# Weight loads that wait for gathered rows, and row numbers copied during a landing wait

## The reference

```
x = x + x-by-feature times w0[cond[b]]             # 64 x 64 matrix chosen per sequence
x = x + attention(x, paged keys and values)         # window of 256, 8 heads, 4 kv heads of 64
x = x + x @ W[id[b]] + b[id[b]]                     # one of 16 experts, 512 x 512 floats each
x = x + x @ W3.T + low-rank term of adapter[b]      # rank 16, one of 8
```

## Time and profile before

| | us |
|---|---|
| median of three timed runs | 1178.34 |
| lowest and highest | 1176.82, 1183.21 |
| profiled execution | 1169.61 |
| its span, first to last instruction | 1167.8 |
| first block | about 0 to 305 |
| second block | about 309 to 1167 |
| TensorE busy | 1050.6 |
| mean granted TensorE clock | 0.950 |

### The profile page before, as it was taken

One profiled execution on the slowest core, in us unless ns is written; L12 is line 12 of the kernel. 1 busy time (PEld: TensorE's weight loads), 2 busy tenths in 40 slices (PEclk: granted clock), 3 DMA queues, 4 the chain that ended last, 5 costly groups with the idle time before them and its releaser, 6 DMA issues. The chain is left out here.

```text
span 1167.8 us, 23800 instructions
## 1 busy us (share of the span) xinstructions
PE 1050.6 (90%) x6440; PEld 713.3 (61%) x6440; DVE 654.7 (56%) x1888; ACT 535.0 (46%) x1336; POOL 535.5 (46%) x597
## 2 busy tenths in 40 slices
PE   4999999999247979999999979999999999999997
PEld 2767677877124655666656646666666666666655
DVE  5889795377333535555555534555555555555552
ACT  3457765475133424544444433444444444444440
POOL 1545444245545454554454445454455554555400
PEclk9999998899666979999999989999999999999998
DMA  3343443353263646665566655656666566665640
GB/s 125 116 137 134 141 147 112 110 167 138 84 198 89 186 149 204 212 214 187 176 205 210 207 168 168 187 182 196 201 227 196 179 201 203 222 195 179 204 145 19
DMA packets 95336, 196.15 MB, mean 168 GB/s; under 512 B 31346, under 2 KB 40114, under 8 KB 87110
## 3 DMA queue, kind: packets, MB, share of 16 engines
q1 hardware_dynamic: 63942, 149.49, 37.9%
q0 software_dynamic: 30784, 44.16, 14.2%
q10 hardware_dynamic: 576, 2.10, 0.5%
HBM read 195.08 MB, written 33.56 MB: 196 GB/s over the span
## 5 line engine op out<-in xcount | busy, mean ns | idle before, releaser
L981 POOL DMA_INDIRECT KV<-kv_scratch,idxs x192 | 190.6, 993 | 290.4 <-DMA KV<-in_pool,idxs 251.4
L971 POOL DMA_INDIRECT KV<-in_pool,idxs x192 | 193.7, 1009 | 107.4 <-issue 81.8
L1130 DVE CUSTOM_DVE_ANT_0 SM<-bank,FM 128x336 f32<-128x336 f32 x256 | 129.8, 507 | 192.8 <-PE bank L1246 171.8
L1052 ACT ACTIVATE PT<-bank 112x384 f32<-112x384 f32 x256 | 111.9, 489 | 264.8 <-PE bank L1254 264.3
L1061 ACT ACTIVATE PR<-SM,nb 128x336 f32<-128x336 f32 x256 | 145.8, 577 | 0.8 <-DVE nb L1134 0.6
L1267 PE MATMUL bank<-PT,KV 112*64 112x128 f32 x1536 | 113.3, 283 | 17.3 <-ACT PT L1052 17.3
L1052 ACT ACTIVATE KT<-bank 128x336 f32<-128x336 f32 x128 | 57.6, 450 | 154.5 <-PE bank L1233 154.5
L1267 PEld LDWEIGHTS bank<-PT,KV 112*64 112x64 f32 x1536 | 86.1, 139 | 65.3 <-issue 40.5
L1292 PE MATMUL bank<-W,XT 128*64 128x512 f32 x512 | 123.7, 604 | 0.7 <-ACT XT L1052 0.7
L90 PE MATMUL bank<-wqh,XTH 128*128 128x512 f32 x256 | 108.0, 422 | 9.2 <-DVE XTL L480 8.5
L1246 PE MATMUL bank<-KT,QB 64*128 64x336 f32 x512 | 111.1, 512 | 5.6 <-ACT KT L1052 5.1
(11 more groups left out here) (157 smaller groups left out, 1934.6 us busy)
## 6 DMA issues: line engine op xcount, KB each, us to landing
W<-in_w SPq DMA_DIRECT2D x64, 1024.0 KB, 8.4
FM<-mask SPq DMA_DIRECT2D x64, 168.0 KB, 4.0
X<-in_x SPq DMA_DIRECT2D x32, 256.0 KB, 2.8
x_scratch<-X SPq DMA_DIRECT2D x32, 256.0 KB, 2.1
kv_scratch<-KVR SPq DMA_DIRECT2D x32, 256.0 KB, 2.5
qt_scratch<-QT SPq DMA_DIRECT2D x32, 256.0 KB, 2.8
QB<-qt_scratch SPq DMA_DIRECT2D x32, 256.0 KB
XB<-x_scratch SPq DMA_DIRECT2D x32, 256.0 KB
```

Of the source, the lines that this page charges most:

```text
L971: pool.indirect_dma_start(out=KV[k][:, c, :], out_offset=None, in_=t["pool"], in_offset=bass.IndirectOffsetOnAxis(ap=idxs[k][:, c:c + 1], ...
L981: pool.indirect_dma_start(out=KV[k][:, c, :], out_offset=None, in_=kv_d, in_offset=bass.IndirectOffsetOnAxis(ap=idxs[k][:, NCH + c:NCH + c ...
L1052: return nc.scalar.activation(dst, src, ACT.Copy)
L1130: v.tensor_tensor_reduce(out=SM[u % 2][:, :], in0=bank[u % 2][:, 0:SPAN], in1=FM[k][:, :], scale=1.0, scalar=-3e38, op0=ALU.add, op1=ALU.m ...
```

## The change

```diff
@@ -950,6 +950,13 @@
 
             @block.gpsimd
             def _(pool):
+                def places(pr, b):
+                    k, n = 2 * pr.par + b, pr.n * 2 + b
+
+                    wait_all(pool, s_pass_pool, (s_new[k], 16 * NCH * pr.i))
+                    nc.gpsimd.tensor_copy(idxs[k][:, :], idxT[:, :, bass.ds(n, 1)].rearrange("p a o -> p (a o)")
+                                          ).then_inc(s_reg[k], 1)
+
                 def body(pr, attention, dense, adapted):
                     if not attention:
                         return
@@ -960,11 +967,7 @@
                         return 8 * (p - 2) + 4 * (b + 1)
 
                     def held(b):
-                        k, n = 2 * pr.par + b, p * 2 + b
-
-                        wait_all(pool, s_pass_pool, (s_new[k], 16 * NCH * pr.i))
-                        nc.gpsimd.tensor_copy(idxs[k][:, :], idxT[:, :, bass.ds(n, 1)].rearrange("p a o -> p (a o)")
-                                              ).then_inc(s_reg[k], 1)
+                        k = 2 * pr.par + b
 
                         wait_all(pool, s_pass_pool, (s_pv, used(b)), (s_reg[k], at(pr.i, 1, 0)))
                         for c in range(NCH):
@@ -983,10 +986,15 @@
                                 in_offset=bass.IndirectOffsetOnAxis(ap=idxs[k][:, NCH + c:NCH + c + 1], axis=0),
                                 bounds_check=NB * T - 1, oob_is_err=False).then_inc(s_new[k], 16)
 
-                    for b in range(2):
-                        held(b)
-                        fresh(b)
-
+                    held(0)
+                    places(pr, 1)
+                    fresh(0)
+                    held(1)
+                    if not last_pair(pr):
+                        places(pr.move(1), 0)
+                    fresh(1)
+
+                places(Pair(0, 0), 0)
                 bodies(pool, body)
 
             @block.sync
@@ -1014,9 +1022,15 @@
                 def body(pr, attention, dense, adapted):
                     p = pr.n
 
+                    def landed(b):
+                        ahead = pr.move(1 + b)
+                        if not (isinstance(p, int) and ahead.n >= PAIRS):
+                            wait(sp, s_old[2 * ahead.par + 1 - b], at(ahead.i, 16 * NCH, 16 * NCH - 1))
+
                     def weights(b):
                         e = sp.value_load(eid[0:1, bass.ds(p * 2 + b, 1)], min_val=0, max_val=E - 1)
                         wait(sp, s_l2, p - 1)
+                        landed(b)
                         sp.dma_start(W2[pr.par][b][:, :], w2_v[bass.ds(e, 1)]).then_inc(s_w2in[pr.par][b], 16)
```

## The result

The changed kernel took 1173.07 us (median of 20 runs, 1164.41 to 1186.32), and the kernel before, run beside it on the same chip, 1184.38 (median of 20, 1176.82 to 1204.67). The ratio is 0.9927, with a 95% interval of 0.9904 to 0.9949: faster by 11 us, where the forecast took off 26.5. The profiled execution took 1164.41 us, 5.2 less than that of before (1169.61); its span is 1162.6.

A forecast was written before the change was run, and what follows sets the result against it. TensorE was taken to be held up by late gathered rows, GpSimd's chain having no slack. Two lone waits and the start, 11.5 + 12.0 + 3 = 26.5 us, off 1178.3 gave 1152, range 1141 to 1174.

The forecast's parts named there:

- What bounds the kernel, and the price of a lone wait: Second block: TensorE waits for late gathered rows; the two lone waits cost 11.5 and 12.0 us, low clock included.
- The copy and the weights' wait: GpSimd's chain and SyncE's weights: 0.8 us saved per half pair, landings 3.3 and 4.0, both lone waits gone, -23.5 us.
- What queues behind that wait: SyncE's queue behind the waiting weights: nothing moves in a steady body; masks land 3.7 to 6.6 us after issue.
- The start: Second block's start: pair 1's rows come earlier, its `scores` at 354 to 357; gains 1 to 4 us, taken as 3.
- The sum: Whole kernel: 11.5 + 12.0 + 3 = 26.5 us off the profiled execution and off the timed median.
- What is late next is TensorE's own work, so undisturbed bodies stay at 24.3 us: Second block's steady stream: with the lone waits gone, TensorE's own work sets each body, 24.3 us.
- Taking the same off gives 1152: Timed median: the 26.5 us taken off 1178.3 leave 1152; forecast chance 0.62.
- the timed runs held more stalls than the profile: Rival, timed runs: the 8.7 us above the profile are nearly one more stall, also removed, giving 1143; chance 0.10.
- The slower case, every gather in a weight's tail: Rival, second block: every gather meets a weight's tail, landings 5.7 us each, bodies 26.4, giving 1211; chance 0.11.

The follow-up runs named there:

- e1: The changed kernel with only the row-number copies moved, the weights not waiting for landings; 1151.18 us, ratio 0.9813 to the kernel before.
- e4: The changed kernel again, unedited, on the first chip; 1142.33 us, ratio 0.9745 to the kernel before.
- e12: The changed kernel with only the row-number copies moved, no weights' wait, on the third chip; 1180.41 us, ratio 0.9992 to the kernel before.
- e2: The changed kernel with only the weights' wait, the row-number copy put back ahead of the old rows; 1175.86 us, ratio 1.0024 to the kernel before.
- e11: The changed kernel a fourth time, unedited, on the third chip; 1173.4 us, ratio 0.9909 to the kernel before.
- e7: The changed kernel a third time, unedited, on the second chip; 1171.88 us, ratio 0.9836 to the kernel before.
- e8: The kernel before, unedited, traced on the second chip; 1185.07 us, ratio 1.0014.
- e9: The changed kernel with weight loads from pair 2 on cut to 256 of 2048 columns; 1176.61 us, ratio 0.9897 to the kernel before.

## Why the prediction was right in its mechanism and wrong in its size

**What bounds the kernel, and the price of a lone wait: right.** The two stalls went; they had cost 35.79 - 24.29 = 11.5 and 36.28 - 24.36 = 11.9 us, and e1 showed a third one of the same price, 11.8.

**The copy and the weights' wait: right as a pair.** GpSimd catches up (18 waits for `values` in e4 against 10 in the earlier trace rows; the 43 of after count longer bodies too), and in e4 the weights stand alone, half a body apart, at 360.89 and 371.56 for the first such pair. The landings of e4 were 3.7 us on average, with 6.3 the longest, where I took 3.3 and 4.0. On the first chip each part alone did less: 26 us off for the copy, none for the wait, 35 for both. On the third the copy alone did nothing (e12).

**What queues behind that wait: right only with the moved copy.** I had found that "in a steady body nothing behind it moves". That held in e4. In e2, with an unmoved copy, queries and masks were issued when they were before, within half a microsecond, but landed late behind a weight that had started 2 us ahead of them, in steady bodies, and the whole gain of the wait was lost.

**The start: wrong, 3 us forecast, none seen.** The first three bodies took 82.56 us in e4 and 82.6 before (324.73 to 407.33). The rows came earlier as worked out, and pair 1's `scores`, forecast for 354 to 357, began at 355.40. What was left out is the body after. The first three bodies of before, then the first and the third of e4:

```profile
324.73:407.33 82.60, 60.93 (x378) 37.56 (x378) 33.84 (x124) 33.14 (x91) 38.23 (x44) 0.78 0.52 160
```

```profile
324.00:355.40 31.40, 17.95 (x84) 10.68 (x83) 9.45 (x37) 11.42 (x29) 18.58 (x21) 0.50 0.41 120
...
380.97:406.56 25.59, 25.20 (x163) 16.51 (x164) 13.17 (x46) 10.97 (x31) 12.56 (x14) 0.94 0.67 191
```

The first body is 1.4 us longer than before (the queries, issued at 347.89), the second 2.8 shorter although it ends in a second wait for queries of 2.41 us, and the third 1.3 longer. That third body has almost no idle time: it runs at a mean granted clock of 0.94 where before had 1.00, right after that second wait. So TensorE stood idle 4.4 us less over the three bodies than before, and was busy 4.3 us longer with the same 378 matmuls at a lower mean clock. I had priced the queue behind the held weight for one body and not for the second, and had put no term for the clock there.

**The sum: 26.5 forecast, 27.0 measured from profile to profile, partly by luck.** e4 against before: the first `scores` 0.7 us earlier, the first four bodies 11.5 less, the next 27 another 11.5, and the end, from the last `scores` on, 3.2. That last term was in no forecast. It is clock alone, the same 270 matmuls at a mean granted clock of 0.93 and of 1.00. Before, then e4:

```profile
1112.68:1167.80 55.12, 45.92 (x270) 31.44 (x269) 20.72 (x61) 13.79 (x37) 0.00 (x0) 0.93 0.23 81
```

```profile
1088.88:1140.80 51.92, 42.73 (x270) 28.86 (x269) 20.73 (x61) 13.79 (x37) 0.00 (x0) 1.00 0.25 87
```

**The step that failed** is "What is late next is TensorE's own work, so undisturbed bodies stay at 24.3 us", together with "Taking the same off gives 1152". On the first chip the first is true, 24.37 us a body, and the median came out even lower than the second says, at 1142.33. In the runs after the prediction, and on two other chips, what was late next was the hand-over from TensorE to ScalarE, VectorE and GpSimd. It made the bodies 25.06 us in after (25.5 in e11: 687.7 us for 27), which is 19 us over 27 bodies more than the 24.36 of the trace that the forecast was made from. Late hand-overs put time into the bodies of either kernel: 27 bodies took 676.7 us in after, 687.7 in e11, 699.9 in e7 (whose profiled execution was its longest), and 688.1 in the kernel before (e8). That alone would leave the difference between the two kernels as it was. What shrinks it is that the longer bodies rescue the chain of before by themselves. In e8 there is one lone stall in place of two, and the copy alone gives a ratio of 0.9992 and not 0.9813. That longer bodies are what takes the stalls away rests on one profile of the kernel before there (e8) and on e12; I haven't lengthened a body on purpose on the first chip to show it.

**The rivals.** That the timed runs held more stalls than the profile (1143) gives the median of the first chip, 1142.33, and there the kernel before is spread from 1164.98 to 1199.57 us and the changed one within 2.3. No trace of a run of before with more stalls was taken on that chip, so its mechanism is not shown. No lone wait for fresh rows was found in the changed kernel's steady stream. The slower case, every gather in a weight's tail, did not come: 64 landing waits took 213.9 us in after, 3.3 each (with the copy's 0.2 us now ahead of the wait), against 251.4 and 3.9 before, and it would have needed 5.7.

## What to carry to other kernels

When a queue is made to wait for a landing, list what stands behind the waiting instruction and move what is needed soonest ahead of it; the version with early queries had the lower median both times that it ran beside the changed kernel (1163.5 against 1171.9 us, 1167.0 against 1173.4), though the intervals overlap. What is issued right behind a large load on the same queue can be late even if it is issued on time (e2). A stall that comes from a chain with no slack seems to be worth its price only where the rest of the kernel is as short as in the profile: where bodies ran 1 us longer, the chain caught up without the change in the one profile of it (e8). So read a second profile of the kernel before, from another chip, before adding up such stalls.

## What the runs showed of the hardware

One program took 1142.33 us on one chip (1141.53 to 1143.82) and 1171.88 and 1173.4 on two others; each chip was seen in one batch only, so chip and hour can't be told apart. In the traces of the two others, and in after, waits behind TensorE end later after the recorded end of the matmul that releases them than on the first chip (for the gathers behind `values` up to 3.0 us and not 1.0), and many of them are put down to "remote". On the first chip no such wait is listed. The granted clock isn't the reason: it is 1.00 in the 27 bodies of after. Nor are the bytes of the 1 MB loads (e9). The long bodies come back at the same places: in all nine traces of that kind the body of pair 8 or of pair 9 takes at least 26.9 us, and in eight of the nine that of pair 27 takes over 26 (in after the bodies of pairs 9, 18 and 27, which start at 557.7, 785.9 and 1010.9, take 27.4, 28.0 and 26.0), with either kernel and with early queries or light weights. That points to something tied to the place in the program or to the time since its start; nothing here tests it, and what it is stays open. The ends of matmuls in a profile are modelled, so the traces can't tell whether the signal is late or the matmuls themselves last longer than recorded. Which chip the runs after the prediction used is not known to me; their times and the trace of after match the second and third, while the trace of before, from which the forecast was made, has no wait on "remote" and bodies of 24.36 us, as on the first.
